# The last 13 of 49 destination blocks summed from gathered rows instead of counts

## The reference

```python
h = jnp.maximum(_layernorm(x, axis=-1), 0.0)
m = jax.nn.relu(h[src]) + 1e-7
ex = jnp.exp(m - seg_max[dst])
a = ex / segment_sum(ex, dst)[dst]
x = x + (h + segment_sum(a * m, dst)) @ W + b
```

## Time and profile before

| | |
|---|---|
| median of three runs | 2484.75 us (2482.11 to 2485.78) |
| the profiled execution, its own time | 2481.58 us |
| its span, first to last instruction | 2479.8 us |
| PE busy | 1859.7 us (75%) |
| DVE busy | 1855.2 us (75%) |
| POOL busy | 1513.4 us (61%) |
| ACT busy | 760.9 us (31%) |
| granted TensorE clock, mean | 0.876 |

### The profile page before, as it was taken

The page is one execution under the profiler, slowest core; times in us unless marked ns, Lnnn a source line. Parts: engine busy times, 40 slices in busy tenths (PEclk is TensorE's granted clock), DMA queues, the critical chain, the costliest instruction groups (busy, mean ns, idle before and its releaser), DMA issues.

```text
span 2479.8 us, 55001 instructions
## 1 busy us (share of the span) xinstructions
PE 1859.7 (75%) x11623; PEld 1549.9 (63%) x11624; DVE 1855.2 (75%) x4293; ACT 760.9 (31%) x1320; POOL 1513.4 (61%) x1559
## 2 busy tenths in 40 slices
PE   3777777767767767667767666767766778999999
PEld 2466656655656556556556555655655666888887
DVE  8999997878878888787878878878878885332333
ACT  5001121222223333334444444544544552000000
POOL 4777777777777777777777777777777712000000
PEclk9899898888888888888888888888888878999999
DMA  5234344444444454444445544544544527566563
GB/s 161 51 83 105 95 117 100 116 115 111 111 112 131 110 132 121 125 126 125 132 125 137 143 129 135 138 134 133 141 133 134 140 84 261 203 218 214 205 219 130
DMA packets 158402, 336.87 MB, mean 136 GB/s; under 512 B 65344, under 2 KB 115546, under 8 KB 142364
## 3 DMA queue, kind: packets, MB, share of 16 engines
q1 hardware_dynamic: 30944, 169.39, 22.7%
q0 software_dynamic: 49248, 75.74, 14.0%
q10 hardware_dynamic: 77990, 89.82, 10.7%
HBM read 244.91 MB, written 89.88 MB: 135 GB/s over the span
## 4 chain that ended last, share of the span: by engine, by line
POOL 54%; PE 20%; issue 18%; DVE 3%; DMA 1%; POOLq 0%; DVEq 0%; ACT 0%; ACTq 0%
POOL rows_buf L542 53%; PE ps L794 15%; DMA rows_buf<-table,index 1%; PE ps L620 1%; PE ps L630 1%; PE ps L722 1%; DVE zone L1311 1%; PE ps L820 1%; DVE planes L1076 0%; DVE ps L1274 0%; PE ps L808 0%; PE ps L776 0%; POOL planes L575 0%; PE ps L802 0%; POOLq L547 0%
## 5 line engine op out<-in xcount | busy, mean ns | idle before, releaser
L542 POOL DMA_INDIRECT rows_buf<-table,index x1539 | 1490.3, 968 | 496.0 <-issue 493.3
L722 PE MATMUL ps<-zone,planes 128*128 128x400 f16 x2352 | 612.6, 375 | 541.2 <-DVE zone L1311 438.7
L1311 DVE TENSOR_SCALAR zone<-iota_c,planes 128x400 f16<-128x400 int16 x2352 | 669.2, 338 | 58.3 <-issue 47.7
L722 PEld LDWEIGHTS ps<-zone,planes 128*128 128x128 f16 x2352 | 250.3, 107 | 721.0 <-issue 663.4
L929 ACT ACTIVATE features_buf<-ps 128x800 f16<-128x800 f32 x392 | 327.8, 836 | 1214.6 <-PE ps L722 1210.9
L620 PEld LDWEIGHTS ps<-wet,zone 128*128 128x128 f32 x3136 | 538.4, 246 | 40.2 <-issue 28.4
L620 PE MATMUL ps<-wet,zone 128*128 128x96 f32 x3136 | 527.1, 326 | 6.5 <-DMA zone<-edge_t 6.5
L607 PE MATMUL ps<-onehot,features_buf 128*96 128x128 f32 x3120 | 427.8, 283 | 0.0
L607 PEld LDWEIGHTS ps<-onehot,features_buf 128*96 128x96 f32 x3120 | 393.9, 173 | 11.9 <-issue 2.0
L1274 DVE TENSOR_TENSOR ps<-ps,rows_buf 128x768 f32<-128x768 f32 x171 | 164.5, 962 | 236.7 <-DMA rows_buf<-table,index 212.7
L1076 DVE TENSOR_TENSOR planes<-ps,planes 128x1536 f16<-128x1536 f32 x196 | 341.4, 1742 | 0.0
(11 more groups left out here) (163 smaller groups left out, 632.1 us busy)
## 6 DMA issues: line engine op xcount, KB each, us to landing
counts<-features_buf ACTq DMA_DIRECT2D x392, 200.0 KB
zone<-edge_t SPq DMA_DIRECT2D x98, 768.0 KB
rows_buf<-counts SPq DMA_DIRECT2D x32, 1600.0 KB, 6.2
single<-table SPq DMA_DIRECT2D x3072, 0.4 KB
planes<-counts SPq DMA_DIRECT2D x17, 1600.0 KB, 6.2
rows_buf<-table,index POOLq DMA_INDIRECT x1539
final<-residual ACTq DMA_DIRECT2D x48, 48.0 KB, 3.0
out<-final ACTq DMA_DIRECT2D x48, 48.0 KB, 3.5
```

Of the source, the lines that this page charges most:

```text
L542: nc.gpsimd.indirect_dma_start(out=into[:, t, :], out_offset=None, in_=table, in_offset=bass.IndirectOffsetOnAxis(ap=at[:, t:t + 1], axis= ...
L722: nc.tensor.matmul(count_ps[:, bass.ds(banks[k], WC)], row_hot[:, u % 2, g * GS + k, :], pair_hot[:, g * GS + k, :], start=False, stop=Fal ...
L1311: last = nc.vector.tensor_scalar(pair_hot[:, k, :], iota_c[:, :], step_pair[:, bass.ds(i * (IS * SC) + (u * SC + k), 1)], None, ALU.is_equal)
```

## The change

The first 36 blocks are summed as before. The last 13 (36 to 48), in which edges are fewest, are summed from one row for each edge:

- SP stores the finished table to DRAM as `weighted` (6250 rows of 768 bytes, 4.8 MB), unit by unit, behind its stores of `hidden`.
- DVE sums `row_sum` by block, PE adds these over the partitions and forms the running sums, and so the number of the first edge of each block reaches SP (`block_start`). SP loads 13 numbers into registers and issues 26 loads of edge lists (source and destination of 15 to 20 times 128 edges from that start).
- POOL gathers the `weighted` rows of those edges, 242 indirect transfers of 128 rows, into two buffers that alternate, each free again when the block two before has been summed.
- DVE builds 242 one-hot matrices 128x128 in fp16 (`fetch_hots`), two slots ahead.
- PE sums such a block with 15 to 20 matmuls instead of 50. The order of blocks is mixed: after the first six, one fetched block follows every two or three counted ones; the last in order is block 48.
- `fast` is 0 also if a block has more edges than its places; the last block may in addition hold the 704 edges that pad the edge list.
- The counts of all blocks are still built and stored. The loops over blocks are written out. `own` and residual of a slot share a semaphore.

```diff
+DB = 36
+GB = NB - DB
+FETCH = [20, 20, 20, 19, 19, 19, 19, 19, 18, 18, 18, 18, 15]
+FETCH_AT = [sum(FETCH[:g]) for g in range(GB + 1)]
+LEAD = 6
+ORDER = []
+for d in range(DB):
+    ORDER.append(d)
+    ORDER.extend(DB + g for g in range(GB) if LEAD + 5 * g // 2 == d + 1)
+assert len(ORDER) == NB
...
+    weighted = nc.dram_tensor("weighted", (N, 4 * D), F16, kind="Internal").ap()
...
+        fetched = [buf[:, 0:max(FETCH) * 2 * D].bitcast(F16).rearrange("p (k d) -> p k d", d=4 * D)
+                   for buf in (zone, features_buf)]
+        fetch_hot = [buf.bitcast(F16)[:, 0:max(FETCH) * P].rearrange("p (k n) -> p k n", n=P)
+                     for buf in (onehot[:, :, :, :].rearrange("p a b c -> p (a b c)"), dstf[:, :])]
...
+        def fetched_before(g):
+            return 16 * sum(FETCH[g % 2:g:2])
...
+                def block_load(b):
+                    sp.dma_start(blocks[b % 3], counts[:, b * BW:(b + 1) * BW, :].rearrange("p w c -> p (w c)")
+                                 ).then_inc(block_in[b % 3], 16)
+
+                block_load(0)
                 sp.wait_ge(node_out, NG)
                 for b in (1, 2):
-                    block_load(b, b)
...
+                sp.wait_ge(starts_ready, 1)
+                for g, start in enumerate(load(sp, block_start, DB, GB, [E] * GB)):
+                    n = FETCH[g]
+                    for buf, edge in ((fetch_src, edge_src), (fetch_dst, edge_dst)):
+                        sp.dma_start(buf[:, FETCH_AT[g]:FETCH_AT[g] + n],
+                                     edge[0:1, bass.ds(start, P * n)].rearrange("a (p k) -> (a p) k", k=n)
+                                     ).then_inc(fetch_in, 16)
                 for u in range(NU):
...
+                for u in range(NU):
+                    sp.wait_ge(exp_high, u + 1)
+                    sp.wait_ge(exp_low, u + 1)
+                    sp.wait_ge(weighted_high, u + 1)
+                    sp.wait_ge(parts_ready, u + 1)
+                    for part in (slice(0, EVEN), slice(EVEN, NP)):
+                        sp.dma_start(weighted.rearrange("(p j) d -> p j d", j=NJ)[part, units[u], :],
+                                     table16[part, units[u], :]).then_inc(weighted_out, 16)
...
+                    sp.dma_start(own[:, b, :], hidden[b * P:(b + 1) * P, :]).then_inc(residual_in[b], 16)
+                for b in range(3, DB):
+                    sp.wait_ge(block_ps, 2 + ORDER.index(b - 3) + 1)
+                    block_load(b)
...
+                pool.wait_ge(fetch_in, 2 * GB * 16)
+                pool.wait_ge(own_out, 2 * NU * 16)
+                pool.wait_ge(weighted_out, 2 * NU * 16)
+                for g in range(GB):
+                    if g >= 2:
+                        pool.wait_ge(block_ps, 2 + ORDER.index(DB + g - 2) + 1)
+                    gather(fetched[g % 2], weighted, fetch_src[:, FETCH_AT[g]:FETCH_AT[g + 1]], fetched_in[g % 2], FETCH[g])
...
-            pe.wait_ge(bad_ready, 2)
-            nc.tensor.transpose(ps[0:1, 6, 0:P], bad[:, 2:3], ident[:, :]).then_inc(bad_ps, 1)
+            pe.wait_ge(bad_ready, 3)
+            nc.tensor.transpose(ps[0:1, 6, 0:P], bad[:, 2:3], ident[:, :])
+            nc.tensor.matmul(ps[0:1, 6, P:P + NB], ones[:, 0:1], in_block[:, :], start=True, stop=True)
...
+            pe.wait_ge(edges_moved, 1)
+            nc.tensor.matmul(ps[0:1, 5, 0:NB], block_edges[:, :], upper[0:NB, 0:NB], start=True, stop=True
+                             ).then_inc(starts_ps, 1)
...
+                def fetched_sums(s, g):
+                    pe.wait_ge(fetched_in[g % 2], fetched_before(g + 2))
+                    pe.wait_ge(fetch_hot_done, g + 1)
+                    pe.wait_ge(soft_done, s + 1)
+                    for k in range(FETCH[g]):
+                        last = nc.tensor.matmul(ps[:, s % 2, 0:4 * D], fetch_hot[g % 2][:, k, :],
+                                                fetched[g % 2][:, k, :], start=(k == 0), stop=(k == FETCH[g] - 1))
                     last.then_inc(block_ps, 1)
...
+                for s in range(2, NB):
+                    if ORDER[s] < DB:
+                        block_sums(s, ORDER[s])
+                    else:
+                        fetched_sums(s, ORDER[s] - DB)
+                    turn(s - 1, s - 1)
+                    finish(s - 2, s - 2)
...
+            nc.vector.tensor_reduce(in_block[:, :], row_sum[:, :].rearrange("p (b k) -> p b k", b=NB), AX.X, ALU.add
+                                    ).then_inc(bad_ready, 1)
...
+            chain(nc.vector.tensor_tensor(block_over[:, :], ps[0:1, 6, P:P + NB], block_room[:, :], ALU.subtract))
+            chain(nc.vector.tensor_reduce(most_over[:, :], block_over[:, :], AX.X, ALU.max))
...
+            chain(nc.vector.tensor_scalar(good[0:1, 2:3], most_over[:, :], 0.0, good[0:1, 1:2], ALU.is_le, ALU.mult))
+            nc.vector.tensor_copy(fast[:, :], good[0:1, 2:3]).then_inc(fast_ready, 1)
+            nc.vector.tensor_copy(block_edges[:, :], ps[0:NB, 7, 0:1]).then_inc(edges_moved, 1)
...
+            dve.wait_ge(starts_ps, 1)
+            nc.vector.tensor_copy(block_start[:, :], ps[0:1, 5, 0:NB]).then_inc(starts_ready, 1)
...
+                def fetch_places():
+                    dve.wait_ge(fetch_in, 2 * GB * 16)
+                    for g in range(GB):
+                        at = slice(FETCH_AT[g], FETCH_AT[g + 1])
+                        nc.vector.tensor_scalar(fetch_at[:, at], fetch_dst[:, at], float((DB + g) * P), None,
+                                                ALU.subtract).then_inc(fetch_at_ready, 1)
+
+                def fetch_hots(g):
+                    dve.wait_ge(fetch_at_ready, g + 1)
+                    if g >= 2:
+                        dve.wait_ge(block_ps, 2 + ORDER.index(DB + g - 2) + 1)
+                    for k in range(FETCH[g]):
+                        last = nc.vector.tensor_scalar(fetch_hot[g % 2][:, k, :], iota_c[:, 0:P],
+                                                       fetch_at[:, FETCH_AT[g] + k:FETCH_AT[g] + k + 1], None,
+                                                       ALU.is_equal)
+                    last.then_inc(fetch_hot_done, 1)
...
-                    dve.wait_ge(own_in[u % BU], (i + (u // BU + 1)) * 16)
+                    dve.wait_ge(residual_in[u % BU], (i + (u // BU + 1)) * 32)
...
+                fetch_places()
...
+                for s in range(2, NB):
+                    for g in range(GB):
+                        if ORDER.index(DB + g) == s + 2:
+                            fetch_hots(g)
+                    softmax(s, s, 0)
+                    add_aggregate(s - 1, (s - 1) % 2)
+                    add_final(s - 2, s - 2, 0, min(P, N - ORDER[s - 2] * P))
```

More of the change, by code:

```diff
@@ L980, in _, with rows_of @@
                 product_high(4)
-                def rows_of(b):
-                    n = P if (b + 1) * P <= N else N - b * P
+                def rows_of(s):
+                    b = ORDER[s]
+                    n = min(P, N - b * P)
                     return n, slice(b * P, b * P + n)
-                def residual_load(b, u, rows_at, n=P, first=False):
-                    if not first:
-                        act.dma_start(own[0:n, u % BU, :], hidden[rows_at, :]).then_inc(own_in[u % BU], 16)
-                    act.dma_start(final[0:n, u % BU, :], residual[rows_at, :]).then_inc(residual_in[u % BU], 16)
```

120 lines of the change are left out of this document (54 added, 66 removed).

## The result

The changed kernel takes 2459.48 us (median of 4 runs, 2456.71 to 2466.66), the kernel before 2484.81 (2482.11 to 2485.78) on the same chip: ratio 0.9906, interval 0.9895 to 0.9918. It is faster by 25 us, about 1%; 58 to 60 us had been forecast. The profiled execution took 2460.79 us, with a span of 2459.0.

A forecast was written before the change was run, and what follows sets the result against it. PE alone was taken to bound the second layer: −66.3 (PE) + 0.2 (last block) + 6.4 (head) + 1.3 (clock) = −58.4 us, giving 2425 us. The range was 2415 to 2450.

The forecast's parts named there:

- PE's gain: Second layer on PE: 13 blocks take 242 matmuls instead of 50 each, 109.7 us down to 43.4, gain 66.3 us.
- A gather's price: GpSimd's new gathers in the second layer: 1.254 us each, 303.5 us for 242, hidden under PE's 330.2 us.
- Rivals 1 and 2: Second-layer gathers slower: 1.35 to 1.55 us makes GpSimd the bound (0.20 including VectorE locking it); from 1.57 no gain (0.06).
- The spare: Second layer: time by which gathered rows land ahead of PE, 7.3 us at fetched block 0, 2.7 at block 1.
- The hots: DVE's 242 one-hot comparisons in the second layer: 0.12 us each, bounds 0.08 to 0.24, unseen by PE.
- Rival 3: Bursts of one-hot comparisons lock GpSimd: 1.5 us each gives 2431, 4.5 gives 2466; 0.20 shared with slower gathers.
- The clock: Before block 2: PE idles some 9 us, then restarts once at the 1.2 GHz level, +1.3 us.
- Some 2,000 us stand as they are: First layer: GpSimd's gathers and the counting that goes with them are untouched by the diff and keep their time.
- The head, (b): Ahead of block 2: SP's 26 edge-list issues at 0.40 us, 10.4 us plus about 1.7 for registers, cost nothing.
- The head, (c): Own rows queue behind weighted stores drained at 410 GB/s; block 2 starts 6.4 us later, second reduce and products included.
- rival 4: Dearer head before block 2: stores at 300 GB/s, issues at 0.7 us, 11 to 17 us; 2428 to 2440; 0.09 beyond range.
- the reduce and the products: Ahead of the second node layer: a second reduce of row_sum and two tiny PE products delay it by 0.8 us.

The follow-up runs named there:

- gathers_beside_again: Kernel before plus 242 GpSimd gathers that nobody reads beside the second layer, where before takes 2484.39 us: 2506.57 us (one run).
- weighted_alone: Changed kernel with all blocks from counts and only the ten weighted stores added: 2499.47 us (one run) against 2489.4 of before.
- changed_again: Changed kernel as it is, measured once more beside the kernel before: 2460.09 us (4 runs), ratio 0.9882.
- lists_alone: Changed kernel with all blocks from counts and only the 26 edge-list loads added: 2494.62 us (one run) against 2489.4 of before.
- own_by_act: Changed kernel with own rows of blocks 0 and 1 loaded by ScalarE's queue: 3840.92 us, ratio 1.037; where before takes 2484.39 us, 2458.19 us, ratio 0.9895.
- gathers_beside: Kernel before plus 242 GpSimd gathers that nobody reads beside the second layer, under the slower conditions: 3985.48 us, ratio 1.0759.
- own_by_act_again: Changed kernel with own rows of blocks 0 and 1 loaded by ScalarE's queue, repeated under the slower conditions: 3824.88 us, ratio 1.0307.
- gathers_two: Kernel before plus two unused gathers behind the second layer's table: 3614.24 us against 3651.57 of before.
- pool_memsets: Kernel before plus 240 small GpSimd memsets in place of added gathers: 3639.71 us against 3651.57 of before.

## Why the prediction was wrong

**PE's gain: right.** 66.3 us were forecast; the stage from block 2 to the end is 65.1 us shorter with block 2's start at a lower clock in it, 66.5 without.

**A gather's price: right.** 1.254 us were taken, from start to start, and 1.26 measured, for rows of twice the bytes. "The pace is set by issuing rows, not by moving bytes" holds as far as bytes go (957 against 955 ns for twice as many); the number of rows was not varied. Rivals 1 and 2 did not come. The spare held: no fetched block of the changed kernel waited. That it was as thin as worked out is seen where block 2 came 13 us sooner and the gather only 3: there PE waited 1.35 us.

**The hots: right, at a somewhat higher price.** 245 ns busy each in the median, about 0.17 us from one to the next in a burst of 20, where 0.12 was taken and 0.08 to 0.24 were the bounds, and no gather above 1.10 us in the stage. Rival 3 did not come there. What looks like its lock did, in the first layer: one gather held to the end of a run of TENSOR_SCALARs. (Rows 10, on which the forecast leaned, show another form: a TENSOR_TENSOR with two inputs in SBUF.) The Trainium skill, SBUF — State Buffer, section "Who interferes with whom", has the second engine fully blocked for the instruction; here it was blocked over some 20 to 25 instructions (31 in gathers_beside_again), while the bursts of hots in the second layer held no gather, so the trace agrees with the rule in part.

**The clock: right, with luck.** +1.3 us forecast for a start after 9 us of idling, 9.69 instead of 8.34 us for block 2's matmuls, after 20 us of it. In other profiles the same 50 matmuls took 9.65 us after 9.8 us of idling, 11.10 after 10.3 (weighted_alone), 10.35 after 5.5 and 10.39 after 21.6 (changed_again): one such start costs 1.3 to 2.8 us here.

**"Some 2,000 us stand as they are": wrong, 24.3 us.** The gathers behind the table make each one ahead of them 11 ns dearer, 17 us of the 21.3, and the held gather is 5 more; about 2.5 us between the last gather and the node layer have no cause that the rows show (from the last gather's start this stretch is 27.1 to 30.4 us long over the profiles under these conditions, and it was 27.1 in the kernel before). gathers_beside_again shows the whole amount, in one run, without any other part of the change. The expectations' 24.7 us contain 0.4 us of the second reduce. No rival had it: the step that failed is the one that took untouched code for unchanged time.

**The head, (b) "Hidden at 0": wrong.** The cover named was that unit 4's features were late anyway. But the stores of units 0 to 3 had used that time, and behind 26 issues they didn't. The issues took 20.2 us, not 10.4 to 12, because two were held, 7.6 us together, with two block loads and the residual ahead of them. lists_alone shows 4.1 us of wait for this step by itself, where 0 was forecast.

**The head, (c): right in kind, too small.** Own rows behind the weighted stores was the choice made, and own_by_act confirms it (9 to 10.5 us come off). The engines drained them at 322 GB/s, not 410, and behind hidden stores whose last issue ended 8.4 us later after the node layer's start than before (52.5 against 44.2). Forecast 5.6 for the head, weighted_alone 9.4, all together 19.1. This is rival 4, and the head alone would have brought about 2439, inside its 2428 to 2440. That is partly luck: it had 11 to 17 us in all against the measured 21 (0.9 + 19.1 + 1.3), with issues at 0.7 us, which didn't come, and late gathers, for which PE did not wait. The first layer's 24.3 us came on top, and took the time out of the range.

**The sum.** Forecast −58.4; then +24.3 for untouched code, +0.1 for the reduce and the products, +13.5 for the head, less 0.3 in the stage: −20.8.

## What to carry to other kernels

Before code is called untouched, ask which engine's program grows: here new gathers at the far end of GpSimd's program made 1539 earlier ones dearer, 21 to 25 us against a gain of 66. A load that is small in bytes is not small on a queue: count its issues, put them against what stands behind them on that queue (not against what they themselves are needed for), and charge a held issue when large transfers are ahead (here 3.3 MB of block loads and 2.4 MB of residual; behind the loads alone none was held). And a head that is made shorter gives only as much as the next late thing lets through: work out the loads and gathers behind it before the time saved is booked.

## What the runs showed of the hardware that was not expected

- An indirect gather of 128 rows takes 940/944 to 947 ns (min/median) where no gather stands behind the table in GpSimd's program, and 951/955 to 952/958 where 242 do; in the other conditions 938/944 to 941/947, and 949/955 to 952/958 with 2 to 480. Memsets in their place or the written-out code of the other engines don't do it.
- In the five profiles of kernels with such gathers, under the conditions of the first result, one gather near 60 us is held until 0.12 us after the end of VectorE's run of TENSOR_SCALARs, over about 21 to 31 of them (6.33, 7.48, 6.56, 6.78 and 8.87 us); in the three without (3.07, 2.25 and 2.32 us at most) none is. In the other conditions none was held beyond 2.5 us either.
- An issue on SP's queue that takes 0.4 us is held up to 5.2 us when two block loads of 1.6 MB and the residual's store are ahead of it.
- In the first twelve runs, where GpSimd gathers while PE multiplies, PE stands still again and again, and the profile shows nothing that it waits for ("issue"; the expectations call it waiting for instructions, which no view here shows): here gathers_beside, PE's timeline.

```profile
3302.84 0.48 PE L806 MATMUL ps<-planes 125*128 125x384 f16 x1 [2.32 <-issue]
3305.64 0.48 PE L806 MATMUL ps<-planes 125*128 125x384 f16 x1 [2.32 <-issue]
```

Single matmuls of 0.48 us stand 2.8 us apart, over 100 times. The variants of the changed kernel have the same gaps there (135.3 us in 123 of them in own_by_act_again, which took 118 us more than the kernel before), and their ratios were 1.0307 to 1.0393. In gathers_beside_again there is no such gap, and none in gathers_two and pool_memsets in the second layer, under the other conditions. A change that moves work to GpSimd beside PE thus gains or loses by conditions that the kernel doesn't choose; what makes them is open.
